# Both normalisations of x1 on GpSimd instead of VectorE, in a two-layer gated cross-attention stack

## The reference, cut to what matters

```
def _layernorm(x, axis=-1, eps=1e-05):
    m = jnp.mean(x, axis=axis, keepdims=True)
    v = jnp.var(x, axis=axis, keepdims=True)
    return (x - m) / jnp.sqrt(v + eps)
...
x = x + jnp.tanh(g_xattn[0]) * _L0_xattn_ref(_layernorm(x, axis=-1), ctx_1024, ...)
x = x + jnp.tanh(g_ffn[0]) * _L0_ffn_ref(_layernorm(x, axis=-1), ...)
x = x + jnp.tanh(g_xattn[1]) * _L1_xattn_ref(_layernorm(x, axis=-1), ctx_1024, ctx_1024, ...)
x = x + jnp.tanh(g_ffn[1]) * _L1_ffn_ref(_layernorm(x, axis=-1), ...)
```

## Time and profile before

| | us |
|---|---|
| median of 3 runs (3772.3 to 3773.69) | 3772.34 |
| the profiled execution | 3774.71 |
| its span | 3772.6 |
| TensorE busy | 3665.2 (97%) |
| VectorE busy | 2636.4 (70%) |
| ScalarE busy | 1711.5 (45%) |
| GpSimd busy | 1386.7 (37%) |

### The profile page before, as it was taken

One profiled execution on the slowest core, in us unless ns is written; L12 is line 12 of the kernel. 1 busy time (PEld: TensorE's weight loads), 2 busy tenths in 40 slices (PEclk: granted clock), 3 DMA queues, 4 the chain that ended last, 5 costly groups with the idle time before them and its releaser, 6 DMA issues.

```text
span 3772.6 us, 95482 instructions
## 1 busy us (share of the span) xinstructions
PE 3665.2 (97%) x34836; PEld 2991.3 (79%) x34836; DVE 2636.4 (70%) x5694; ACT 1711.5 (45%) x3115; POOL 1386.7 (37%) x1333
## 2 busy tenths in 40 slices
PE   7999999999999999999999999999999999999998
PEld 5778878878878878878878878878878878878865
DVE  4676776776776776776776776776776776776775
ACT  4444444444444444444444444444444444444431
POOL 3333433433433433433433433433433433433323
PEclk9999999999999999999999999999999999999999
DMA  3000000000000000000000000000000000000001
GB/s 96 11 14 16 12 12 16 12 12 16 12 12 16 12 12 16 12 13 16 12 13 16 11 13 16 12 13 16 12 13 16 11 13 16 11 13 16 11 26 65
DMA packets 58916, 64.83 MB, mean 17 GB/s; under 512 B 5344, under 2 KB 55808, under 8 KB 58240
## 3 DMA queue, kind: packets, MB, share of 16 engines
q10 hardware_dynamic: 34688, 32.52, 2.8%
q1 hardware_dynamic: 24192, 31.81, 2.6%
HBM read 47.01 MB, written 17.30 MB: 17 GB/s over the span
## 4 chain that ended last, share of the span: by engine, by line
PE 91%; DVE 6%; ACT 1%; issue 1%; POOL 0%; SPq 0%; DMA 0%; DVEq 0%; ACTq 0%; POOLq 0%
PE g L818 28%; PE g L824 17%; PE scores L818 12%; PE scores L921 6%; PE g L971 6%; DVE xn L1177 4%; PE g L887 4%; PE g L990 3%; PE scores L955 3%; PE scores L981 3%; PE g L838 3%; PE scores L925 2%; PE g L898 1%; DVE kT_lo L1207 1%; ACT kT_hi L663 1%
## 5 line engine op out<-in xcount | busy, mean ns | idle before, releaser
L761 ACT ACTIVATE prob<-scores 120x1024 f32<-120x1024 f32 x512 | 498.5, 1023 | 509.0 <-PE scores L925 438.4
L1316 DVE SCALAR_TENSOR_TENSOR x<-g,lg_w,x 128x256 f32<-128x256 f32 x1024 | 494.8, 483 | 250.3 <-PE g L818 226.7
L597 POOL TENSOR_TENSOR q_lo<-an,q_hi 128x512 fp32r<-128x512 f32 x256 | 331.7, 1308 | 278.0 <-ACT q_hi L790 278.0
L818 PE MATMUL g<-ew_hi,yT_hi 128*128 128x512 f32 x1024 | 426.5, 416 | 0.0
L818 PE MATMUL g<-ew_lo,yT_hi 128*128 128x512 f32 x1024 | 401.7, 392 | 0.0
L818 PE MATMUL g<-ew_hi,yT_lo 128*128 128x512 f32 x1024 | 399.5, 390 | 0.0
L1255 DVE TENSOR_REDUCE y_nm<-g 128x4 f32<-128x480 f32 x512 | 301.0, 650 | 110.6 <-PE g L898 110.6
L542 POOL TENSOR_TENSOR y_rstd<-y_mv,eps 128x2 f32<-128x2 f32 x128 | 25.0, 195 | 960.7 <-DVE y_mv L1172 960.7
L1255 DVE TENSOR_REDUCE x_nm<-g 128x4 f32<-128x480 f32 x512 | 313.1, 654 | 82.6 <-PE g L887 82.6
L592 POOL TENSOR_TENSOR q_lo<-q_full,q_hi 128x512 fp32r<-128x512 f32 x256 | 330.3, 1299 | 65.3 <-ACT q_full L695 65.3
L542 POOL TENSOR_TENSOR x_rstd<-x_mv,eps 128x2 f32<-128x2 f32 x64 | 12.5, 195 | 886.1 <-DVE x_mv L1172 886.1
(11 more groups left out here) (213 smaller groups left out, 9540.8 us busy)
## 6 DMA issues: line engine op xcount, KB each, us to landing
x_in<-in_x ACTq DMA_DIRECT2D x64, 256.0 KB, 2.8
out<-y_x SPq DMA_DIRECT2D x64, 256.0 KB, 2.1
ctx_in<-in_ctx ACTq DMA_DIRECT2D x128, 120.0 KB, 2.3
wk_s<-in_gu SPq DMA_DIRECT2D x8, 512.0 KB, 3.4
vx<-in_ew SPq DMA_DIRECT2D x2, 1024.0 KB, 5.0
wk_s<-in_wk SPq DMA_DIRECT2D x1, 1024.0 KB, 5.2
prob<-in_wq SPq DMA_DIRECT2D x1, 1024.0 KB, 7.7
wv_s<-in_wv SPq DMA_DIRECT2D x1, 1024.0 KB, 10.4
```

Source lines behind the costliest of these rows:

```text
L597: g.tensor_tensor(q[1][:, 2 * h:2 * h + 2, :], an[:, 2 * (h % 2):2 * (h % 2) + 2, :], q[0][:, 2 * h:2 * h + 2, :].bitcast(F32), ALU.subtra ...
L761: a.activation(prob[:, e].rearrange("p o u s -> p (o u s)"), scores[0:NK, banks, :].rearrange("p o c -> p (o c)"), ACT.Exp, scale=scale).t ...
L818: ins = t_.matmul(out_, lhsT[u], rhs[v], start=first and n == 1, stop=last and n == 3 * len(terms))
L1316: ins = v.scalar_tensor_tensor(out=x1[:, t, :], in0=ring.bank(Y_FFN[j])[:, o * D:(o + 1) * D], scalar=lg_w[:, t, 2 * n + o:2 * n + o + 1], ...
```

## The change

GpSimd, which computes the power, also makes xn from x1, at both places. VectorE's steps `p_norm` and `y_norm3` are gone from its program and from the tables; `n_norm` stays with VectorE.

```
+            def normalise():
+                pool.drain()
+                for t in range(T):
+                    ins = g.tensor_scalar(xn[:, t, :], x1[:, t, :], y_mv[:, t, 0:1], y_rstd[:, 1, t:t + 1],
+                                          ALU.subtract, ALU.mult)
+                ins.then_inc(y_normed.sem, 1)
...
             def y_norm2(i, _):
+                if not first(i):
+                    ring.full(pool, i - 1, Y_TR3)
                 rstd(y_mv, y_rstd, y_stats, 2, y_rs, 0, i)
+                normalise()
 
             def y_stat3(i, _):
+                if not (isinstance(i, int) and i + 2 >= B):
+                    ring.full(pool, i + 2, X_TR)
                 rstd(y_mv, y_rstd, y_stats, 4, y_rs, 2, i)
+                normalise()
...
-            def p_norm(i, _):
-                y_rs.wait(dve, i, 2)
-                normalise(x1, y_mv, y_rstd, xn, y_normed)
-
             def y_stat3(i, _):
                 ring.all_empty(dve, i, Y_FFN[6:8])
                 statistics(x1, y_st6, y_mv, y_stats)
-
-            def y_norm3(i, _):
-                y_rs.wait(dve, i, 4)
-                normalise(x1, y_mv, y_rstd, xn, y_normed)
```

The two new waits of GpSimd are there because xn is one buffer: at place A the transposes `y_tr3` of the batch before, at place B those of `n_tr` must have read it. In the tables only the two names are taken out, as in this line of `ORDER`:

```
-    ("y_maxt", 0), ("n_q", 0), ("n_k", 1), ("n_q", 1), ("y_maxt", 1), ("p_norm", 0), ("n_q", 2), ("p_load", 0),
+    ("y_maxt", 0), ("n_q", 0), ("n_k", 1), ("n_q", 1), ("y_maxt", 1), ("n_q", 2), ("p_load", 0),
```

More of the change, by code:

```diff
@@ L53 @@
     ("n_tr", 0), ("y_ffn", 7), ("y_stat3", 0), ("x_sum", 0), ("x_pv", 0), ("x_mul", 0), ("x_mul", 1), ("x_hi", 0),
-    ("y_norm3", 0), ("x_mul", 2), ("x_mul", 3), ("x_pv", 1), ("x_pv", 2), ("x_hi", 1), ("x_sum", 1), ("x_pv", 3),
+    ("x_mul", 2), ("x_mul", 3), ("x_pv", 1), ("x_pv", 2), ("x_hi", 1), ("x_sum", 1), ("x_pv", 3),
     ("y_tr3", 0), ("z_out", 0), ("x_hi", 2), ("y_v", 0), ("n_ctx", 0), ("y_q", 0), ("x_hi", 3), ("n_k", 0),
     ("x_out", 0), ("y_max", 0), ("x_out", 1), ("x_out", 2), ("y_max", 1), ("y_res", 0), ("x_out", 3), ("p_stat", 0),
-    ("y_maxt", 0), ("n_q", 0), ("n_k", 1), ("n_q", 1), ("y_maxt", 1), ("p_norm", 0), ("n_q", 2), ("p_load", 0),
+    ("y_maxt", 0), ("n_q", 0), ("n_k", 1), ("n_q", 1), ("y_maxt", 1), ("n_q", 2), ("p_load", 0),
     ("p_tr2", 0), ("n_q", 3), ("n_max", 0), ("y_st", 0), ("n_max", 1), ("p_gate", 0), ("n_v", 0), ("p_lg", 0),
@@ L72 @@
         ("x_mul", 2), ("x_mul", 3), ("x_pv", 2), ("x_hi", 2), ("x_hi", 3), ("x_pv", 3), ("n_k", 0), ("n_tr", 0),
-        ("n_k", 1), ("x_out", 0), ("x_out", 1), ("x_out", 2), ("x_out", 3), ("p_stat", 0), ("n_q", 0), ("p_norm", 0),
+        ("n_k", 1), ("x_out", 0), ("x_out", 1), ("x_out", 2), ("x_out", 3), ("p_stat", 0), ("n_q", 0),
         ("n_q", 1), ("n_q", 2), ("p_tr2", 0), ("p_load", 0), ("n_q", 3), ("n_res", 0), ("n_max", 0), ("p_gate", 0),
@@ L80 @@
         ("x_st", 2), ("y_ffn", 3), ("n_norm", 0), ("y_ffn", 4), ("y_ffn", 5), ("y_ffn", 6), ("y_ffn", 7),
-        ("y_stat3", 0), ("n_tr", 0), ("x_pv", 0), ("x_sum", 0), ("y_norm3", 0), ("x_mul", 0), ("x_st", 3), ("x_pv", 1),
+        ("y_stat3", 0), ("n_tr", 0), ("x_pv", 0), ("x_sum", 0), ("x_mul", 0), ("x_st", 3), ("x_pv", 1),
         ("x_mul", 1), ("x_hi", 0), ("x_mul", 2), ("x_hi", 1), ("x_mul", 3), ("y_res", 0), ("x_sum", 1), ("x_pv", 2),
@@ L84 @@
         ("n_k", 0), ("n_v", 0), ("x_out", 0), ("y_max", 0), ("x_out", 1), ("x_out", 2), ("y_max", 1), ("x_out", 3),
-        ("p_stat", 0), ("n_q", 0), ("y_maxt", 0), ("n_k", 1), ("n_q", 1), ("y_maxt", 1), ("n_q", 2), ("p_norm", 0),
+        ("p_stat", 0), ("n_q", 0), ("y_maxt", 0), ("n_k", 1), ("n_q", 1), ("y_maxt", 1), ("n_q", 2),
         ("p_tr2", 0), ("n_q", 3), ("y_st", 0), ("n_max", 0), ("p_gate", 0), ("n_max", 1), ("y_st", 1), ("n_max", 2),
@@ L93 @@
         ("x_st", 2), ("y_ffn", 6), ("y_ffn", 7), ("y_stat3", 0), ("x_sum", 0), ("x_st", 3), ("x_pv", 0), ("m_coef", 2),
-        ("x_mul", 0), ("x_hi", 0), ("x_pv", 1), ("x_mul", 1), ("x_sum", 1), ("x_pv", 2), ("m_norm", 0), ("y_norm3", 0),
+        ("x_mul", 0), ("x_hi", 0), ("x_pv", 1), ("x_mul", 1), ("x_sum", 1), ("x_pv", 2), ("m_norm", 0),
         ("x_hi", 1), ("x_pv", 3), ("m_coef", 3), ("x_mul", 2), ("x_mul", 3), ("m_tr", 0), ("y_tr3", 0), ("z_out", 0),
@@ L97 @@
         ("y_res", 0), ("x_out", 1), ("x_out", 2), ("y_max", 1), ("x_out", 3), ("p_load", 0), ("p_stat", 0),
-        ("m_bias", 0), ("m_gu", 0), ("y_v", 0), ("p_ctx", 0), ("y_maxt", 0), ("y_maxt", 1), ("p_norm", 0), ("p_tr2", 0),
+        ("m_bias", 0), ("m_gu", 0), ("y_v", 0), ("p_ctx", 0), ("y_maxt", 0), ("y_maxt", 1), ("p_tr2", 0),
         ("p_gate", 0), ("y_st", 0), ("p_lg", 0), ("m_gu", 1), ("y_st", 1), ("y_mul", 0), ("y_pv", 0), ("p_wt", 0),
@@ L103 @@
         ("m_sig", 0), ("y_ffn", 0), ("y_ffn", 1), ("z_hi", 1), ("y_k", 0), ("y_ffn", 2), ("y_ffn", 3), ("m_sig", 1),
-        ("y_ffn", 4), ("y_ffn", 5), ("y_ffn", 6), ("y_ffn", 7), ("y_stat3", 0), ("y_norm3", 0), ("m_gu", 2),
+        ("y_ffn", 4), ("y_ffn", 5), ("y_ffn", 6), ("y_ffn", 7), ("y_stat3", 0), ("m_gu", 2),
         ("y_tr3", 0), ("m_sig", 2), ("z_out", 0), ("y_v", 0), ("m_dnw", 1), ("m_gu", 3), ("m_dnw", 0), ("y_q", 0),
@@ L1406, in m_gate_up @@
                 v.tensor_scalar(m_u[n % 2], m_u[n % 2], -LIMIT, 1.0, ALU.max, ALU.add).then_inc(m_up, 1)
-            run(dve, {"n_stat": n_stat, "n_norm": n_norm, "p_stat": p_stat, "p_norm": p_norm, "y_stat3": y_stat3,
-                      "y_norm3": y_norm3, "n_tr": x_tr, "n_k": x_k,
+            run(dve, {"n_stat": n_stat, "n_norm": n_norm, "p_stat": p_stat, "y_stat3": y_stat3,
+                      "n_tr": x_tr, "n_k": x_k,
                       "x_mul": x_mul, "y_mul": y_mul, "p_tr2": y_tr(Y_TR2, 1), "y_tr3": y_tr(Y_TR3, 3), "y_k": y_k, "y_q": y_q,
```

## The result

| | before | changed |
|---|---|---|
| median | 3772.32 us | 3908.13 us (3907.09 to 3908.8, 4 runs) |
| ratio | | 1.0359, 95% interval 1.0341 to 1.0377 |
| span of the profiled execution | 3772.6 us | 3905.4 us |
| length of one batch in the loop | 56.60 us | 58.77 us |

The change makes the kernel slower by 136 us, 2.17 us per batch. The forecast was 3719 us, range 3710 to 3768.

The account below looks back on a forecast made before the run. TensorE, busy 97%, was taken as the bound; ending its 0.93 us wait for xn, less GpSimd's delays, wins 0.83 us per batch, 53 us over 64: 3772.34 to 3719 us, range 3710 to 3768.

Parts of the forecast that it names:

- Where the kernel is bound: TensorE, busy 97% of the span; only its idle time, under 1 us per batch, can be won.
- place A: Normalisation behind p_stat: TensorE's p_tr2 wait for xn goes, 0.93 us per batch won; 2(X - 0.43) lost through n_max 1.
- X: Time of one GpSimd subtract-and-multiply of 128x256: taken as 0.48 us, bounds 438 and 741 ns.
- the first kind: GpSimd operations with one input, such as the affine select, 0.83 ns per element; source of the low end, 438 ns.
- The drain: GpSimd's drain between the power and xn, put at 0.07 us.
- Place B: Normalisation behind y_stat3: no TensorE wait to win; delayed q_lo holds up y_q, losing 2(X - 0.49) us per batch.
- The sum: Per batch 0.93 - 2(X - 0.43) - 2(X - 0.49), each from where positive: 0.83 us, times 64 53 us.
- Rival (2): GpSimd about half as fast as VectorE, X = 0.78: n_max 1 and y_q wait, 3795 us; chance 0.11.

Follow-up runs that it names:

- e6_ahead_held: Kernel before with p_norm moved ahead of n_k 1 in the loop's table and GpSimd held behind its power until VectorE has made xn: 3719.10 us, ratio 0.9856.
- e3_prices: Kernel before with 18 GpSimd instructions, nine forms run twice, added in its start-up to price them; the change's instruction took 1224 ns.
- e4_half: The change with the second of the two GpSimd xn instructions left out at both places, output unusable: 3754.21 us, ratio 0.9949 against the kernel before.
- e8_broadcast: The change with xn made by two GpSimd TENSOR_TENSOR over both tiles, mean and power read as broadcast columns: 3851.01 us, ratio 1.0214 against the kernel before.
- e5_ahead: Kernel before with only p_norm moved ahead of n_k 1 in the loop's table, GpSimd unchanged: 3805.91 us, ratio 1.0085.

## Why the prediction was wrong

- **Where the kernel is bound, and the wait of place A**: right. `e6_ahead_held` gives 0.86 to 0.90 us per batch for it, the prediction took 0.93.
- **X, the failed step**: the sentence "it is nearest to the first kind" took GpSimd's affine select, 0.83 ns per element, for the neighbour of a subtract-and-multiply. That operation takes 3.34 ns per element, and X is 1.22 us in place of 0.48. The high end of 741 ns, from TENSOR_TENSOR, was also too low: I had taken the form with two inputs as a bound from above on the one with one, and `e3_prices` shows the reverse (850 against 725 ns with one step). The rows could not exclude it: two starting points 4 and 8 elements wide say nothing of a slope, and the only large one-input row was another operation. The estimate by the Trainium skill (GPSIMD Engine Reference, section 3.1 Elementwise), 445 ns, fell with it: its 1.03 cycles per element at 1.2 GHz are 0.86 ns, and the measured 3.34 decides.
- **The drain**: 0.19 us, not 0.07; 0.12 us at each place, 15 us in all.
- **Place A**: right in mechanism. With the measured delay of 2.60 us and the offset of 0.03 by which `q_lo` used to start ahead of the power's end, `n_max 1` would be late by 1.69 us. Against the 0.90 won that leaves 0.79; measured 44.5 us over 64, 0.70. The wait for xn, which was to be gone up to X = 1.2, is still there with 0.2 us, since X came out above that.
- **Place B**: right in mechanism, 1.58 by the sum against 88.1 us over 64, 1.38; 0.08 of the difference is the pair of `q_lo`, 2.54 us in place of 2.62. With X over some 0.86 a wait for xn itself comes ahead of the one for `yT_lo`: in `e4_half`, where they do not wait, the transposes start 2.03 us behind the power's end (1514.97 to 1517.00), and that less the hop of 0.13 and the drain of 0.19 is 2X. The two waits lie one behind the other in the same delay, and the total is that of the later. "TensorE did not wait here" was not exact either: before, VectorE's xn ended at 1525.51 and the transposes started at 1525.64, which is the hop of 0.13, and 1.12 us behind the start of the group of products ahead of them, where `e4_half` has 0.97. The list of waits does not show these 0.15 us, since the records of that group run to 1525.57.
- **The sum**: 0.93 - 1.69 - 1.58 = -2.34 us per batch from the prediction's own terms, 150 us; measured 2.17 in the loop and 136 us.
- **Rival (2)** named the mechanism, the side and the point from which it decides (X = 0.69), and was given 0.11 and too small a size (X = 0.78, 3795 us), by the same mistake.

## What to carry to other kernels

An operation that no row of the trace shows at its size has no upper bound from another form: run it alone at two sizes, in some idle stretch, before a forecast or a rewrite rests on it. When work moves to an engine with idle time, what counts is the work queued behind it: here, once the room of some tenths of a us was used up, each us in GpSimd's queue cost TensorE a us at either place, in waits of TensorE for ScalarE and VectorE. And where two engines slow each other, it can be cheaper to hold the one with room for 0.9 us than to move the work: that was one name and one wait, for 55 us.

## What the runs showed of the hardware that I had not expected

- On GpSimd (`e3_prices`, each form run twice), TENSOR_SCALAR in fp32 is slower than TENSOR_TENSOR: 850 ns for 256 elements with one constant step against 725 ns with a full second tensor; by slope 2.50 ns per element with one step and 3.33 with two. A second input that is a broadcast column makes TENSOR_TENSOR cheaper still: 507 ns for 192 elements, 1.04 us for 512 (`e8_broadcast`).
- The affine select (292 ns for 128 elements) is no measure for any of these.
- A drain on GpSimd behind the power costs 0.19 us; without it the next instruction started 0.03 us ahead of the power's end.
- VectorE's two xn instructions take 0.74 us with GpSimd idle and 3.18 us when they start beside `q_lo` with `kmx` behind it. GpSimd's own instructions hardly notice: `kmx` takes 1784 to 1846 ns in `e5_ahead` and 1780 to 1796 in `e6_ahead_held`.
